# Zero fills of the slot arrays issued one stage earlier, and semaphores cleared by ranges

## The reference, cut to what matters

```python
x = x + L0_xattn(layernorm(x), ctx)      # cross attention, one head
x = x + L0_attn(layernorm(x), ...)       # causal self attention, 16 heads of 64
x = x + L0_ffn(layernorm(x), ...)        # 16 experts, top 4, and a shared expert
x = x + L1_xattn(layernorm(x), ctx, ctx) # cross attention, 16 heads of 32
x = x + L1_attn(layernorm(x), ...)       # self attention, low rank weights
x = x + L1_ffn(layernorm(x), ...)        # 8 experts, top 2
```

## Time and profile before

| | us |
|---|---|
| profiled execution | 2125.66 |
| its span | 2123.9 |
| timed runs, median | 2127.68 |
| TensorE busy | 1743.3 (82%) |
| VectorE, GpSimd, ScalarE busy | 842.9, 799.3, 595.0 |

### The profile page before, as it was taken

One profiled execution on the slowest core, in us unless ns is written; L12 is line 12 of the kernel. 1 busy time (PEld: TensorE's weight loads), 2 busy tenths in 40 slices (PEclk: granted clock), 3 DMA queues, 4 the chain that ended last, 5 costly groups with the idle time before them and its releaser, 6 DMA issues. The chain is left out here.

```text
span 2123.9 us, 38357 instructions
## 1 busy us (share of the span) xinstructions
PE 1743.3 (82%) x13882; PEld 1406.2 (66%) x13882; DVE 842.9 (40%) x1659; ACT 595.0 (28%) x1213; POOL 799.3 (38%) x540
## 2 busy tenths in 40 slices
PE   6786898944899981899999999878762799999993
PEld 5444777733688860788888888755552577878782
DVE  4445353546333345133333323345455322323333
ACT  2112241522233312233333333326343211111110
POOL 0003223106488524433333333222103199785502
PEclk8996999977899995999999999977686899999997
DMA  6672001067577535211111111010007355453303
GB/s 238 232 279 85 21 1 60 1 231 298 173 230 240 169 113 159 71 42 31 31 38 30 40 30 40 2 45 7 26 14 281 151 180 187 149 174 111 99 21 128
DMA packets 97164, 236.68 MB, mean 111 GB/s; under 512 B 9712, under 2 KB 26736, under 8 KB 97040
## 3 DMA queue, kind: packets, MB, share of 16 engines
q1 hardware_dynamic: 68768, 172.84, 23.9%
q10 hardware_dynamic: 20592, 36.98, 5.1%
q0 software_dynamic: 7680, 25.17, 3.5%
HBM read 183.58 MB, written 51.38 MB: 111 GB/s over the span
## 5 line engine op out<-in xcount | busy, mean ns | idle before, releaser
L128 PE MATMUL banks<-ra_DE 128*128 128x258 f32 (+2 forms) x912 | 321.6, 353 | 30.1 <-ACT fa_DE L2100 8.4
L129 PE MATMUL banks<-ra_DE 128*128 128x258 f32 (+2 forms) x912 | 312.0, 343 | 0.0
L130 PE MATMUL banks<-ra_DE 128*128 128x258 f32 (+2 forms) x912 | 311.6, 342 | 0.0
L128 PE MATMUL banks<-weights_F,rest_r_F 128*128 x552 | 227.2, 412 | 13.0 <-ACTq L1641 10.4
L128 PEld LDWEIGHTS banks<-ra_DE 128*128 128x128 f32 (+1 forms) x912 | 177.6, 195 | 62.8 <-ACT fa_DE L2100 14.1
L130 PE MATMUL banks<-weights_F,rest_r_F 128*128 x552 | 218.2, 395 | 0.0
L129 PE MATMUL banks<-weights_F,rest_r_F 128*128 x552 | 217.7, 394 | 0.0
L130 PEld LDWEIGHTS banks<-ra_DE 128*128 128x128 f32 (+1 forms) x912 | 178.2, 196 | 19.3
L129 PEld LDWEIGHTS banks<-ra_DE 128*128 128x128 f32 (+1 forms) x912 | 178.5, 196 | 16.1
L1597 POOL TENSOR_TENSOR weights_F<-rest_F,weights_F 128x1536 fp32r<-128x1536 f32 x52 | 181.8, 3496 | 4.2
L2067 POOL TENSOR_TENSOR fa_DE<-fa_DE 128x1028 f32<-128x1028 f32 x32 | 60.8, 1901 | 254.5 <-DVE fa_DE L2163 254.5
(11 more groups left out here) (460 smaller groups left out, 3343.1 us busy)
## 6 DMA issues: line engine op xcount, KB each, us to landing
rest_F<-in_L_units SPq DMA_DIRECT2D x52, 768.0 KB, 4.2
rest_C<-in_L_units SPq DMA_DIRECT2D x30, 768.0 KB, 4.9
fa_DE<-in_ctxT SPq DMA_DIRECT2D x32, 514.0 KB, 4.0
e_sorted<-temps_C SPq DMA_DIRECT2D x1, 12032.0 KB, 37.8
rest_C<-e_sorted ACTq DMA_DIRECT2D x47, 256.0 KB, 3.5
ea_y_scratch<-rest_C ACTq DMA_DIRECT2D x47, 256.0 KB, 3.0
tail_F<-in_L_units SPq DMA_DIRECT2D x12, 768.0 KB, 17.7
fa_AB<-in_ctxT SPq DMA_DIRECT2D x16, 514.0 KB, 9.7
```

The source lines that it names most:

```text
L128: pe.matmul(psum, lh, rh, start=first, stop=False)
L129: pe.matmul(psum, lh, rl, start=False, stop=False)
L130: return pe.matmul(psum, ll, rh, start=False, stop=last)
```

## The change

The zero fill of each expert layer moves into the loop block of the second half of the self attention before it, and its zeroed tile is written by `constants`. The clears take a range of numbers each.

```diff
+def routed_tiles(layer):
+    return ((K0, K1)[layer] * T + (E0, E1)[layer] * (P - 1)) // P
...
 def free_semaphores():
             with nc.Block() as block:
                 @block.sync
                 def _(eng):
-                    for s in layer_sems:
-                        eng.sem_clear(s)
+                    numbers = sorted(s.num for s in layer_sems)
+                    while numbers:
+                        n = next((n for n, v in enumerate(numbers) if v != numbers[0] + n), len(numbers))
+                        eng.sem_clear(range(numbers[0], numbers[0] + n))
+                        numbers = numbers[n:]
...
+        sorted_rows = [nc.dram_tensor(f"e{layer}_sorted", [routed_tiles(layer) * P, D], F32, kind="Internal").ap()
+                       for layer in range(2)]
+        s_zeroed = [gather_sem(f"e{layer}_zeroed") for layer in range(2)]
...
             def constants(eng):
+                pool.memset(zeros[:], 0.0)
                 for u in range(2):
                     pool.memset(pb[u], 0.0)
...
                 if hh == 0:
                     @block.sync
                     def _(eng):
                         following[0][0](eng)
+                else:
+                    @block.sync
+                    def _(eng):
+                        layer = int(low_rank)
+                        eng.dma_start(sorted_rows[layer].rearrange("(j p) d -> p j d", p=P), zeros[:].unsqueeze(1)
+                                      .to_broadcast([P, routed_tiles(layer), D])).then_inc(s_zeroed[layer], 16)
...
             def load_gate(eng, _):
...
-                eng.wait_ge(s_zeros, 1)
-                eng.dma_start(plan.sorted.rearrange("(j p) d -> p j d", p=P),
-                              zeros.unsqueeze(1).to_broadcast([P, J, D])).then_inc(plan.s_zeroed, 16)
...
             def gate_lows(eng, _):
                 pool.memset(gate, 0.0).then_inc(s_clear, 1)
-                pool.memset(zeros, 0.0).then_inc(s_zeros, 1)
...
-                    fa, na = area("fa", [P, F_SIZE]), area("na", [P, N_SIZE])
+                    fa, na, zeros = area("fa", [P, F_SIZE]), area("na", [P, N_SIZE]), area("zeros", [P, D])
```

More of the change, by code:

```diff
@@ L1223, in __init__ @@
                 self.layer, self.experts, self.choices = layer, (E0, E1)[layer], (K0, K1)[layer]
-                self.routed = (self.choices * T + self.experts * (P - 1)) // P
+                self.routed = routed_tiles(layer)
                 self.shared = NT if layer == 0 else 0
@@ L1250, in __init__ @@
                 self.s_fill = [sem(f"e{layer}_filled{n}") for n in range(self.preloaded, self.slots)]
-                self.s_zeroed, self.s_scattered = gather_sem(f"e{layer}_zeroed"), gather_sem(f"e{layer}_scattered")
-                self.sorted = nc.dram_tensor(f"e{layer}_sorted", [self.routed * P, D], F32, kind="Internal").ap()
+                self.s_zeroed, self.s_scattered = s_zeroed[layer], gather_sem(f"e{layer}_scattered")
+                self.sorted = sorted_rows[layer]
             def place(self, n):
@@ L1275, in routing @@
             gate_high, gate_low, kept = r.take(DC, P), r.take(DC, P), r.take(NT, E)
-            zeros = f.take(D)
             gate, gbias = f.take(DC, P), f.take(E)
@@ L1290, in routing @@
                                             "kept", "links"))
-            s_zeros = sem(f"{tag}_zeros")
             def compare(links, v, n, dst):
```

## The result

The changed kernel ran in 2102.56 to 2111.36 us, median 2105.8 us of 4 runs, against 2129.88 us for the kernel before in the same comparison. The ratio is 0.9906, with a 95% interval of 0.9883 to 0.9929: 1% faster. By this ratio the time fell by 20 us (15 to 25); the two medians alone would give 0.9887. The forecast was 2109 us in a range of 2102 to 2123. The profiled execution's span is 2102.4 us, 21.5 us less.

What follows compares the result with a forecast made beforehand. Three gaps between parts, 21.85 us, where SP alone clears semaphores, were taken as on the path. 2125.66 - 18.4 = 2107.2 us profiled, with the fill and clock at 0; the median runs 2.0 above: 2109 us, range 2102 to 2123.

Steps and rivals of the forecast that it cites:

- The gap is SP's row of clears, and all of it is on the path: Between parts, SP alone clears semaphores while other engines wait at the barrier; all 21.85 us is on the path.
- three gaps as one line: DVE's gaps between parts (9.17, 4.08, 8.60 us) grow linearly with clears, 0.0572 us each.
- the 30 ns of the row: Lower price per clear, its reported duration on SP; if only that were saved, the gain is 9.7 us.
- the 0.99 us: Rest of each gap between parts once its clears are taken off, given to the two barriers and branches.
- 322 clears fewer are 18.4 us: At the three part ends, 8 clears replace 330; at 0.0572 us each this gains 18.4 us.
- A range has the price of one clear: At the part ends, a clear of many semaphores was taken to cost the same as a single clear.
- Rival 1: At the part ends, ranges cost per semaphore: time stays at 2128 us, chance 0.08; half-way form 2118, chance 0.07.
- 27 of 57: Of each clear's 57 ns on SP, 27 lie outside execution; used to argue the cost is mostly per instruction.
- Rival 2: At the three part boundaries, the next part's code comes late, 2.0 us each, 6 us in all: 2115; chance 0.12.
- The fill had time to spare: In routing, the zero fill was early by 4.0 and 11.2 us, so moving it gains 0.
- Rival 3: In the self attention loop, the moved fill holds up instruction code, ending 21 us slower at 2148; chance 0.03.
- The clock, plus or minus 3 us: TensorE's clock recovery in routing varies by itself, up to 1.6 us each; taken as 0 with 3 us either way.

Runs made afterwards that it cites:

- e1: The kernel before with only the clears taken by ranges, zero fills left in routing: 2105.52 us, ratio 0.9895 to before.
- e7: The kernel before with only the clears taken by ranges, run again beside the changed kernel on one chip: 2106.0 us, ratio 0.9905.
- e5: The kernel before with every single clear issued twice, 660 in all: 2148.43 us, ratio 1.0105.
- e2: The changed kernel with the loop of single clears put back, so the moved fill alone: 2127.66 us, ratio 1.0003 to before.
- e4: The changed kernel with a second zero fill of the same size behind the first, into its own array: 2111.28 us, ratio 0.9930.
- e6: The kernel before with as many clears, 330, each taking the whole run of numbers its own lies in: 2183.7 us, ratio 1.0275.
- e3: The changed kernel run again without any edit: 2108.93 us, ratio 0.9920 to the kernel before.
- e8: The changed kernel without any edit, run again beside the ranges alone on one chip: 2104.79 us, ratio 0.9906 to before.

## Why the prediction was right

**The gap is SP's row of clears, and all of it is on the path.** Shown three ways: taking the clears away alone gave the gain (e1, e7), doubling them gave 61 ns each on the path (e5), and putting the single clears back took the gain away (e2). The reading of three gaps as one line, rather than the 30 ns of the row, decided between 2109 and 2118 us; e5 settles it by its own gaps.

**The line through the three gaps was right by some luck.** The row of the clears can be read more closely. Those of AB in the kernel before, in two windows of time (434 to 440.8 and 440.8 to 444 us):

```profile
L111 SPq EVENT_SEMAPHORE_RANGE_CLEAR  x97: 25/30/43, 435.0 to 440.6; - x97
L111 SPq EVENT_SEMAPHORE_RANGE_CLEAR  x46: 25/30/31, 441.0 to 443.6; - x46
```

One clear follows the other every 58 ns, and once in the row SP pauses for some 0.4 us more, here between 440.6 and 441.0. The rows of C and DE have one such pause each too (834.2 to 834.6 and 1584.7 to 1585.1 us). Three rows of unlike counts with one pause each lie on one line, and the line puts the pause to what is left of a gap. So of the 0.99 us that the prediction gave to the two barriers and branches some 0.4 were the pause; from the first start to the last end the rows take 8.61, 3.51 and 8.04 us, and beside them a gap has 0.56 us before and 0.58 after. In e5 the row of AB has two pauses, 128 clears apart (441.8 and 449.5 us), and so has that of DE (1599.2 and 1606.9), whose first clear also starts 0.3 us later than before; C's has one. This is what lies above the line there. The longer gap of e4 is such a pause too, between two clears of DE. What SP waits for in it, no run here shows: an instruction that arrives late would look like this, but that is not shown.

**322 clears fewer are 18.4 us.** The gaps gave 19.1. The term was 0.7 us small: 322 times 58 ns are 18.7 us, the three pauses that went with the clears are some 1.1 more, and the ranges take 0.6 us back.

**A range has the price of one clear.** This was taken from the instruction's name and was not quite so. The widest range takes 276 ns for one number's 31 [the row of L117 above], (276 - 31) / 142 = 1.7 ns for each further number, and e6 shows the same on the path. Rival 1, a price by the number, was right in kind and wrong in size by a factor of 30: the eight ranges with their 329 numbers run 0.6 us longer than eight single clears. So the forecast was little touched by it. What the prediction set against this rival, that the 57 ns are "mostly" outside execution, does not follow from its own 27 of 57.

**No code comes late at a shorter gap.** Rival 2 expected 2 us at each end. A gap has the same 0.56 to 0.58 us beside its clears before and after, so no engine waits longer there than it did. The Trainium skill has a taken branch stall only where its target is not held ("Runtime: NRT & Kernel Launch", section "Instruction fetch mechanics"); no such stall shows at these ends, and whether the code was held there no run shows.

**The fill had time to spare and still has.** It was moved from a place where it cost nothing to another where it costs nothing. It landed near 396.5 and 1523.9 us, 4 and 12 us earlier than forecast: in AB the transfer itself was shorter (34.7 us for 37.8), in DE the block began 13.5 us earlier than in the kernel before, whose start the forecast had used. The memset, 525 ns in the new place, is covered: POOL still idles 27.59 us behind its work in AB and 7.08 in DE. Rival 3 did not come: four packets of code moved beside the fill of AB, and even 24 MB in one loop lengthened it by only some 0.3 us (e4).

**The clock, plus or minus 3 us.** This was the right size and explains a part of the rest. That all up to 434 us stands where it stood came true to 0.8 us, by chance: between executions of kernels that are the same up to there, parts differ by 1 us and more. DVE's first instruction of AB's second norm stands at 175.1 us before and at 178.2 in e1, which have the same code up to that point, and AB ended between 432.8 and 437.4 us in the ten. So C, DE and F begin 9.1, 12.5 and 22.7 us earlier for 8.1, 11.0 and 18.4 forecast; the last is off by 0.7 us of gaps and 3.6 us of the parts' own lengths, of which F gives back 1.2. That these fell on the good side here is luck.

In DE one place can be read. The same 8 us of the second half's loop in the kernels before, after, and with the ranges alone (columns as above):

```profile
1529.00:1537.00 8.00, 7.58 (x91) 6.14 (x92) 2.94 (x7) 4.56 (x10) 0.53 (x2) 0.50 0.00 0
```

```profile
1514.90:1522.90 8.00, 7.03 (x101) 5.69 (x103) 3.10 (x8) 4.96 (x10) 0.54 (x2) 0.73 0.91 335
```

```profile
1518.20:1526.20 8.00, 7.21 (x103) 5.85 (x105) 3.16 (x8) 4.82 (x10) 0.53 (x2) 0.72 0.00 0
```

TensorE stays at 1.2 GHz for the whole stretch in the first (0.50) and comes back to 2.4 GHz within it in the other two (0.73 and 0.72), with the fill beside it in one and no DMA at all in the other. This stretch of DE, from the second half's first projection copy on, is 1.0 us shorter in both. So of DE's 2.6 us 1.0 is the clock, and not the fill. The other place is routing in F, where the change lost time. The 24 gate matmuls of F in the changed kernel, to be held against the earlier trace rows:

```profile
1577.80:1585.30 7.50, 7.02 (x24) 5.41 (x24) 0.00 (x0) 0.35 (x1) 0.00 (x0) 0.81 0.00 0
```

They take 7.02 us at 0.81 of full clock with no DMA beside them, and took 5.72 at 1.00 beside the fill. That bears out the prediction's reading that the clock and not the traffic makes this difference. The ten profiled executions in us, the gap ahead of DE, the stretch of DE without its gap, and DVE's way through routing of F, from its first instruction of the part to the drain:

| execution | fill moved | gap ahead of DE | stretch of DE | routing of F |
|---|---|---|---|---|
| before | no | 4.08 | 78.9 | 29.5 |
| after, e3, e8 | yes | 0.88 | 77.9 | 30.8 to 30.9 |
| e1, e7 | no | 0.87, 0.88 | 77.9 | 30.9 |
| e2 | yes | 4.02 | 78.9 | 31.1 |
| e4 | twice | 0.88 | 78.9 | 29.5 |
| e5, e6 | no | 7.17, 6.84 | 77.9 | 31.1, 31.0 |

Each place has two values, and neither value goes with the fill or with the length of the gap: e5 and e6 have the longest gaps and the short stretch of DE, e4 a short gap and the long one. They go with the granted clock. Over the same 8 us of DE it is 0.50 in the three long ones (before, e2, e4) and 0.71 to 0.73 in the other seven; at F's gate matmuls it is 1.00 in before and e4 and 0.77 to 0.81 in the other eight. What decides which of the two an execution gets stays open.

The other 1.6 us of DE stay open too. DE as a whole took 741.4 to 742.8 us in the five executions with a short gap ahead and the short stretch, 743.9 and 743.8 in e5 and e6, and 745.2 to 745.4 in the three with the long stretch. So it may be that a long gap ahead of DE costs 1 to 2 us within it; e4, with a short gap and 745.2 us, speaks against that.

## What to carry to other kernels

Where all engines meet at a barrier and one of them then runs a row of tiny instructions, the whole row is on the path, and it shows in no busy share: look for gaps that all engines have at once, and for the count of the instruction that the last engine runs in them. Price such a row by its first and last start or by the difference between gaps of unlike counts, since the duration in the row of the instruction can be half of its pitch; then look for pauses within the row, which a line through the gaps hides. A transfer that has slack where it stands gains nothing by an earlier start; read its landing against the instruction that ends the stage before moving it.

## What the runs showed of the hardware that was not expected

- Single clears of semaphores follow one another every 58 ns on SP, though each is shown as 25 to 43 ns, and the row pauses for 0.3 to 0.4 us more once in each of the three rows of before, and 128 clears apart where a row has two pauses (e5).
- A clear of a range of semaphores runs 31 ns for one number, 98 for 41, 205 for 102 and 276 for 143 in the kernel after: near enough 1.7 ns for each further number, against 58 ns for each single clear. One range fits less well, 104 ns for 29 numbers.
- A 12 MB write of zeros from SBUF to DRAM, at 356 GB/s and with the DMA engines 95% busy, did not lengthen a 72 us loop of matmuls, copies and vector work by anything that can be told from executions without it; 24 MB lengthened it by some 0.3 us.
